# Query and key rows of an attention + mixture-of-experts block: loaded whole, by the sync queue, beside the expert tiles

## What is computed

```
x: [2, 1024, 256];  xn = layernorm(x)
y = x + attention(xn) + ffn(xn)
attention: qkv = xn @ qkv_w.T + qkv_b; 16 heads of 16; scores = q.k/4 + slope*(k_pos - q_pos), causal softmax; @ v; @ out_w.T + out_b
ffn: scores = sigmoid(xn @ gate_w); the top 2 of 16 experts by scores + expert_bias, weights normalised to sum 1
     shared  = (silu(xn @ sg_w) * (xn @ su_w)) @ sd_w
     routed  = sum over the two experts e of weight_e * ((silu(g) * u) @ experts_down[e]),  [g|u] = xn @ experts_gate_up[e]
     ffn     = shared + routed
```

## Time and profile before

| | us |
|---|---|
| median of 3 executions | 526.53 |
| lowest, highest | 524.24, 529.89 |
| the profiled execution | 525.04 |
| its span, first to last instruction | 523.2 |
| TensorE busy in it | 461.9 (88%) |
| VectorE busy | 324.3 (62%) |
| ScalarE busy | 249.4 (48%) |
| POOL busy | 198.4 (38%) |
| HBM read, written | 37.27 MB, 27.13 MB |

### The profile page before, as it was taken

One profiled execution on the slowest core, in us unless ns is written; L12 is line 12 of the kernel. 1 busy time (PEld: TensorE's weight loads), 2 busy tenths in 40 slices (PEclk: granted clock), 3 DMA queues, 4 the chain that ended last, 5 costly groups with the idle time before them and its releaser, 6 DMA issues.

```text
span 523.2 us, 9031 instructions
## 1 busy us (share of the span) xinstructions
PE 461.9 (88%) x3049; PEld 271.6 (52%) x3050; DVE 324.3 (62%) x610; ACT 249.4 (48%) x567; POOL 198.4 (38%) x239
## 2 busy tenths in 40 slices
PE   4595999737859999995999999999999999999998
PEld 4454788525635666763445354444444444332676
DVE  3869985413425656676867877778586867744232
ACT  2620652112213333332767676676676757678300
POOL 3470777699940000006888888800000000000000
PEclk9799799977779999997999999999999999999999
DMA  9898999799999434424113333221120000010022
GB/s 282 188 403 256 318 323 291 246 170 144 188 174 203 127 110 121 130 79 140 42 49 104 108 86 106 71 76 61 48 82 18 3 3 3 1 13 6 3 89 73
DMA packets 65705, 64.60 MB, mean 123 GB/s; under 512 B 21935, under 2 KB 59539, under 8 KB 65635
## 3 DMA queue, kind: packets, MB, share of 16 engines
q1 hardware_dynamic: 51506, 47.85, 30.9%
q0 software_dynamic: 13056, 15.83, 15.0%
q10 hardware_dynamic: 1104, 0.41, 0.3%
HBM read 37.27 MB, written 27.13 MB: 123 GB/s over the span
## 4 chain that ended last, share of the span: by engine, by line
PE 66%; DVE 13%; DMA 12%; issue 2%; ACT 2%; POOL 2%; SPq 1%; POOLq 0%; DVEq 0%
PE ps L1248 12%; PE ps L1222 10%; PE ps L1234 10%; PE ps L1147 7%; PE ps L1268 5%; DMA x_in<-sorted_tokens 5%; DVE mx L970 5%; PE ps L1043 4%; PE ps L1163 4%; DMA ks<-aux_rows 2%; PE ps L1237 2%; PE ps L1223 2%; PE ps L1137 2%; ACT pt L718 2%; DMA x_sb<-x 1%
## 5 line engine op out<-in xcount | busy, mean ns | idle before, releaser
L718 ACT ACTIVATE pt<-ps 128x512 f32<-128x512 f32 (+3 forms) x384 | 167.1, 494 | 79.7 <-PE ps L1237 55.2
L970 DVE TENSOR_REDUCE mx<-ps 128x1 f32<-128x384 f32 (+6 forms) x189 | 153.3, 863 | 52.4 <-PE ps L1223 51.1
L1248 PE MATMUL ps<-pt,vg 128*32 128x512 f32 (+3 forms) x768 | 71.9, 492 | 0.0
L575 POOL DMA_INDIRECT yg<-sorted_outputs,slot_i x32 | 32.0, 1000 | 94.2 <-DMA sorted_outputs<-y_out 85.4
L1147 PE MATMUL ps<-w_gu,hx 128*128 x192 | 58.3, 432 | 3.8 <-issue 2.2
L1234 PE MATMUL ps<-qs,ks 111*128 111x512 bf16 (+3 forms) x192 | 55.7, 331 | 3.7 <-DMA qs<-nr 3.0
L1234 PE MATMUL ps<-qk 111*128 111x512 bf16 (+3 forms) x192 | 54.9, 329 | 1.8 <-ACT pt L718 0.3
L935 DVE COPY y_out<-ps 128x256 f32<-128x256 f32 x48 | 20.4, 425 | 56.4 <-PE ps L1163 52.7
L1237 PE MATMUL ps<-cbf 128*128 128x128 bf16 x256 | 52.4, 221 | 0.0
L691 ACT ACTIVATE hx<-ps 128x384 f32<-128x384 f32 (+1 forms) x48 | 22.9, 477 | 61.3 <-PE ps L1137 58.6
L1222 PE MATMUL ps<-qk 108*128 108x512 bf16 (+3 forms) x192 | 50.2, 328 | 1.8 <-DVE mx L970 1.3
(11 more groups left out here) (175 smaller groups left out, 737.9 us busy)
## 6 DMA issues: line engine op xcount, KB each, us to landing
sorted_tokens<-y_out SPq DMA_DIRECT2D x12, 512.0 KB, 5.0
qk_parts<-parts SPq DMA_DIRECT2D x16, 384.0 KB, 3.5
x_in<-sorted_tokens SPq DMA_DIRECT2D x48, 128.0 KB, 2.7
sorted_outputs<-y_out SPq DMA_DIRECT2D x48, 128.0 KB, 1.7
w_gu<-e_gu SPq DMA_DIRECT2D x1, 2816.0 KB, 12.9
x_sb<-x SPq DMA_DIRECT2D x4, 512.0 KB, 8.4
w_dn<-e_dn SPq DMA_DIRECT2D x1, 2048.0 KB, 8.7
y<-x_sb SPq DMA_DIRECT2D x16, 128.0 KB, 1.7
```

The costliest lines, as they stand in the source:

```text
L575: g_.indirect_dma_start(out=yg[:, n % 4, :], out_offset=None, in_=ysd, in_offset=bass.IndirectOffsetOnAxis(ap=slot_i[:, k, t:t + 1], axis= ...
L718: sc.activation(pt[:, s % 4, j, lo:CH], bank(n % 3)[:, lo:CH], ACT.Exp).then_inc(s_exp, 1)
L970: last = v.reduce_max(dst, src, axis=AX.X)
L1248: ins = te.matmul(ps[32 * j:32 * j + 32, OUT_BANK * CH + lo:(OUT_BANK + 1) * CH], vg[:, par, kb, j, :], pt[:, s % 4, j, lo:CH], start=kb = ...
```

## The change

`load` becomes `load_piece(queue, g, piece)`, which issues one transfer of a whole row (all 1024 positions, 8 KB in a partition): a list `ROW_PIECES` numbers the eight of a group. The two halves' semaphores become one per group. SP issues the eight of group 0 after the second part of the gate/up weights and before it waits for the scattered tokens, behind waits for the last shared-expert product (`s_g1`) and the last job (`s_free`). The loop of SP over tiles is written out, and behind the store of each of the tiles 0 to 23 it issues one piece of the groups 1 to 3. POOL issues none any more, and its waits ahead of them go. Groups 4 to 7 are loaded by SP at the same place, with eight transfers instead of sixteen. TensorE waits once per group.

```diff
--- before.py
+++ after.py
@@ -314,8 +314,8 @@
         s_ga = [sem(f"rows_gathered{i}") for i in range(4)]
         s_gw = sem("rows_weighed")
         s_gad = sem("rows_added")
-        s_first = [[sem(f"first_half{half}_loaded{n}") for n in range(NBUF)] for half in range(2)]
-        s_ld = [[sem(f"half{half}_loaded{n}") for n in range(NBUF)] for half in range(2)]
+        s_first = [sem(f"first_rows_loaded{n}") for n in range(NBUF)]
+        s_ld = [sem(f"rows_loaded{n}") for n in range(NBUF)]
         s_vg = sem("vg_ready")
         s_fr = sem("first_max_scores_ready")
         s_ff = sem("first_max_scores_read")
@@ -360,23 +360,25 @@
         LOADS = 8
         SC = HD ** -0.5
 
-        def load(queue, side, g, half):
-
+        ROW_PIECES = [(side, t0, n) for side in range(2) for t0, n in ((0, 3), (3, 2), (5, 1), (AUX0, 0))]
+
+        def load_piece(queue, g, piece):
+
+            side, t0, n = ROW_PIECES[piece]
             dst, order = (q_buf, k_buf)[side][g % NBUF], (Q_PARTS, K_PARTS)[side]
-            done = (s_first, s_ld)[g // NBUF][half][g % NBUF]
-            cols = slice(half * CH, (half + 1) * CH)
-            for t0, n in ((0, 3), (3, 2), (5, 1)):
+            done = (s_first, s_ld)[g // NBUF][g % NBUF]
+            if n == 0:
+                rows = (N_ALIBI, N_AUX)[side]
+                queue.dma_start(dst[AUX0:AUX0 + rows, :, :],
+                                auxd[side, g:g + 1, :, 0:rows, :].rearrange("g j r s -> r (g j) s")
+                                ).then_inc(done, DMA)
+                return
+            if side == 0:
                 p0 = order[t0]
-                if side == 0:
-                    src = qkd[0, p0:p0 + 1, g:g + 1, :, :, cols].rearrange("n g d j s -> (g n) d j s")
-                    src = src.broadcast_to([n, HD, HG, CH])
-                else:
-                    src = qkd[1, 0:n, g:g + 1, :, :, cols].rearrange("n g d j s -> (g n) d j s")
-                queue.dma_start(dst[HD * t0:HD * (t0 + n), :, cols], src).then_inc(done, DMA)
-            rows = (N_ALIBI, N_AUX)[side]
-            queue.dma_start(dst[AUX0:AUX0 + rows, :, cols],
-                         auxd[side, g:g + 1, :, 0:rows, cols].rearrange("g j r s -> r (g j) s")
-                         ).then_inc(done, DMA)
+                src = qkd[0, p0:p0 + 1, g:g + 1].rearrange("n g d j s -> (g n) d j s").broadcast_to([n, HD, HG, S])
+            else:
+                src = qkd[1, 0:n, g:g + 1].rearrange("n g d j s -> (g n) d j s")
+            queue.dma_start(dst[HD * t0:HD * (t0 + n), :, :], src).then_inc(done, DMA)
 
         @block.sync
         def _(sp):
@@ -437,6 +439,11 @@
             sp.dma_start(w_gu[:, 0:E_LATE, :, :], e_gu[0:E_LATE].rearrange("e (c p) f -> p e c f", p=P)
                          ).then_inc(s_wgu, DMA)
 
+            sp.wait_ge(s_g1, 4)
+            sp.wait_ge(s_free, NJ)
+            for piece in range(LOADS):
+                load_piece(sp, 0, piece)
+
             sp.wait_ge(s_scat, K_TOP * TT * DMA)
 
             def load_tile(k, u):
@@ -460,10 +467,11 @@
 
             for k in range(4, 7):
                 next_tile(k, k % 4)
-            with sp.Fori(0, NT // 4 - 2) as i:
-                for u in range(4):
-                    next_tile(i * 4 + u + 7, (u + 3) % 4)
-                    store_tile(i * 4 + u, u)
+            for k in range(NT - 8):
+                next_tile(k + 7, (k + 3) % 4)
+                store_tile(k, k % 4)
+                if k < (NBUF - 1) * LOADS:
+                    load_piece(sp, 1 + k // LOADS, k % LOADS)
             next_tile(NT - 1, 3)
             for k in range(NT - 8, NT):
                 store_tile(k, k % 4)
@@ -479,9 +487,8 @@
                     store_neg(g + 1, (g + 1) % 2)
                 if g + NBUF < NG:
                     sp.wait_ge(s_st, (g + 1) * (HG * NS))
-                    for half in range(2):
-                        for side in range(2):
-                            load(sp, side, g + NBUF, half)
+                    for piece in range(LOADS):
+                        load_piece(sp, g + NBUF, piece)
 
             for g in range(NG):
                 sp.wait_ge(s_rec, max(0, g - (NG - 3)) + 1)
@@ -551,16 +558,6 @@
             pool.wait_ge(s_free, NJ)
             copy_v(0, 0)
             copy_v(1, 1)
-
-            pool.wait_ge(s_sh, TT // 2)
-            pool.wait_ge(s_auxst, 4 * DMA)
-            for i, stored in enumerate(s_parts):
-                pool.wait_ge(stored, DMA * len(range(i, NQK, RING)))
-            pool.wait_ge(s_scat, K_TOP * TT * DMA)
-            for g in range(NBUF):
-                for half in range(2):
-                    for side in range(2):
-                        load(pool, side, g, half)
 
             for u in range(4):
                 pool.wait_ge(s_ys[u], NT // 4 * DMA)
@@ -1165,8 +1162,8 @@
 
             def first_scores(j, q, n, first):
 
-                if first and n in (0, QT // 2):
-                    pe.wait_ge(s_first[n // (QT // 2)][0], LOADS * DMA)
+                if first and n == 0:
+                    pe.wait_ge(s_first[0], LOADS * DMA)
                 if not (first and n == 0):
                     pe.wait_ge(s_ff, n)
                 w = (q + 1) * P
@@ -1286,16 +1283,15 @@
                                 weigh(g + par - (a == 0), (a - back) % NS, par - (a == 0))
                         elif kind == "max" and not (last and a + par > 1):
                             n = g + par + a
-                            if b in (0, FIRST_HALF):
-                                pe.wait_ge((s_first, s_ld)[n // NBUF][int(b > 0)][n % NBUF], LOADS * DMA)
+                            if b == 0:
+                                pe.wait_ge((s_first, s_ld)[n // NBUF][n % NBUF], LOADS * DMA)
                             max_scores(n, n % 2, b)
                 for s in (NS - 2, NS - 1):
                     weigh(g + 1, s, 1)
                 return beside
 
 
-            for half in range(2):
-                pe.wait_ge(s_first[half][1], LOADS * DMA)
+            pe.wait_ge(s_first[1], LOADS * DMA)
             for p in range(EARLY):
                 max_scores(1, 1, p)
             for g in range(0, NG, 2):
```

## The result

| | median us | lowest, highest | executions |
|---|---|---|---|
| before | 525.38 | 523.81, 529.89 | 4 |
| changed | 564.85 | 564.33, 566.08 | 4 |

The changed kernel takes 1.074 times as long, with a 95% interval of 1.067 to 1.081: 39.5 us slower, where 20.5 had been forecast. The profiled execution of it has a span of 562.8 us against 523.2.

The account below looks back on a forecast made before the run. TensorE held two thirds of the chain, with transfers setting the pace between 99 and 160 us. Store 28 came 21 us later, the rest added zero: 525.04 + 21 = 546, on the median's scale 547; range 531 to 561.

Parts of the forecast that it names:

- The engine count: Sync-queue q/k loads: transfers of three or two repeats run on three or two of sixteen DMA engines; 23 us a group.
- step 2: Groups 1 to 3 beside 24 tiles: the most loaded DMA engine is the bound, 85.4 us, 3.6 us a tile.
- step 3: After the last piece: store 28 leaves about 2 us later, at 219 instead of 197.95, +21 us.
- step 1: Group 0 ahead of the tiles: drain from 98 to 121, first transposes 121.5 (+21 us), store 0 at 131.5.
- The tail: Tile steps 28 to 47: run as before, since nothing crowds them today.
- step 4: Groups 4 to 7, loaded beside attention: TensorE waits for no q/k row there; zero change.
- A: Whole q/k rows: all sixteen engines share them, 4.4 us a group; -20 us, 506.5; 9 in 100.
- B: Sync queue: tile loads overtake the q/k pieces; -9 us, 517; 3 in 100.
- C: Q/k loads: long runs are faster than allowed, 31 GB/s from an engine; time 527; 6 in 100.
- D: Sync queue: blocks on issue and stores slip behind pieces, 26 us a group; +35, 561; 12 in 100.
- The signs: Tile stage: DMA share some 0.2 with TensorE idle, transposes near 121, stores 3.6 us apart, tile-load waits 35 us or more.

Follow-up runs that it names:

- wide_all: Changed kernel with the sixteen dimensions outermost and repeats inside, in source and SBUF, for all eight groups; 507.92 us, ratio 0.968 to the kernel before.
- the ladder: Changed kernel, then the same with large transfers' outer source count raised to 4, 8 and 16; 564.85, then 534.4, 517.5 and 507.9 us.
- spread_40: Changed kernel with the 24 pieces of groups 1 to 3 behind 24 of the first 40 stores instead of the first 24; 565.80 us.
- one_big: Changed kernel with a two- or three-repeat piece behind every third or fourth store and a small one behind the next, over 40 stores; 559.35 us.
- group0_behind: Changed kernel with group 0 issued behind the first four tile loads instead of ahead of them; 556.91 us.
- lone_big: As one_big, but the twelve small pieces of groups 1 to 3 go behind the last eight stores; 560.71 us.

## Why the prediction was right in its direction and short in its size

**The engine count** was the whole argument, and it held: the earlier trace rows showed three and two engines, wide_all and the ladder prove it for the whole rows too. The mechanism was right. The time lies 4 us above the range, because terms of the sum were too small: above all the queue's 85.4 us of step 2, then the 2 us of step 3 and the start of step 1. Before to after by these marks:

| | predicted | measured |
|---|---|---|
| store 0 leaves (step 1) | 131.5 | 135.54 |
| from there until the queue is through with its pieces: landing of the load of tile 31 (step 2) | 85.4 | 94.5 |
| from there to store 28 (step 3) | 2 | 7.4 |
| store 28 leaves | 219 | 237.46 |

**Step 1**, short by 4. The first transposes came at 126.02 instead of 121.5. Of these 4.5 us, 2.1 are the profiled execution's own earlier stages (weights issued at 87.63 instead of 85.55), 1.3 a longer landing of the weights (14.2 instead of 12.9 us), and 1.1 the drain, 24.1 against 23 us. On its plateaus an engine ran faster than I took it, 27 GB/s, but not throughout: from 104 to 108 us a share of 0.19, three engines, moved only 58 GB/s. Store 0 then came 9.5 us later, where I had 10.

**Step 2**, short by 9, is the term that missed most. That the engine never runs dry and is the bound is borne out by the landings, which follow each other without a gap; the beat is 15.1 us for four tiles, 3.77 a tile, where I had 3.6. But a piece was priced at its bytes, 131 kB / 24 = 5.5 us and 0.3 for the load behind it. The first one took 10.8 us, 5 more; the other eleven took 66.5 us, 2.6 more; the tiles' own traffic makes the rest. Counting bytes per engine works while the pieces are packed. spread_40 and one_big show where it fails: with the queue empty in between, each piece of three repeats costs some 4 us more, and the mean load forecasts a gain that doesn't come.

**Step 3**, short by 5, let the load of tile 31 gate store 28, 2 us ahead of it. That load landed at 230.1, but the gate in the trace is the load of tile 29, the last one behind a large piece. From its landing at 228.15 to store 28 at 237.46 are three steps after a wait, at a granted clock of 0.57 from 230 to 235 us, 9.3 us in all. The pieces that end the queue are small, and TensorE, once let go, must still do every tile between the gate and the mark, at the lower clock first.

4 + 9.1 + 5.4 = 18.5, which is 237.46 - 219. The tail was right to 0.1 us, and **step 4** was right as well: no wait for a q/k row in attention.

**The rivals.** A's price was in effect a forecast of wide_all: 506.5, measured 507.92. That it came so near is in part luck: group 0 took 9.5 us there instead of 4.4 and store 0 left at 120.66 instead of 112.5, and the tiles behind it took 2.14 us instead of 2.34. For the changed kernel A did not happen; B did not either (group0_behind shows an order kept), nor C. D, with 561, was near in number only: its bubbles aren't in the landings.

**The signs** named at the end came true, with one proviso: DMA share 0.26 with TensorE idle, first transposes in the 120s, stores 3.7 us apart from store 5 to 28, no wait at the first scores. TensorE's waits on tile loads are 50.7 us where "35 or more" stood, but only with the first one; beside the pieces alone they are 25. Every term that missed, missed to the same side, and the range above 547 should have been the wider side.

## What to carry to other kernels

Before a transfer is moved to the sync queue, look at what rate that queue gives the same shape: a plateau that is a small multiple of the rate of one engine (here 27 GB/s) with a DMA share of a few sixteenths says that the outermost count of the source (3 or 2) sets the number of engines. The remedy is the order of the dimensions, not the place or the size of the transfer: with a count of 16 outermost the same moves went from 7% slower to 3% faster, and a count of 8 already had 47 of the 57 us. And price what stands ahead of a small, urgent transfer in the same queue as a delay to be set against its buffers' cover, one large piece at a time, not as a mean load. Where pieces can't be spread over all engines, spreading them in time isn't a way out: over 40 tiles instead of 24 they won nothing, or 1% at most.

## What the runs showed of the hardware that I had not expected

- With all sixteen engines on q/k rows (wide_all, share 0.99) only 185 GB/s moved, while the clearing stores moved 405 at the same share. So group 0 took about 9.5 us where 4.4 were reckoned. Each transfer there writes 16 to 48 partitions; whether that is the cause wasn't tried.
- A tile load right behind one three-repeat transfer with nothing large ahead landed 10.1 to 11.5 us after issue (one_big, lone_big), where the bytes ahead of it and its own landing make 7; behind other pieces the same transfer added only 6.0 to 6.9 us (changed kernel). Not explained.
- Each engine's rate fell when more of them worked on q/k rows: 27 GB/s with two and four, 25 with three, 14 to 20 with eight, 11.6 with sixteen.
- Longer runs did raise the rate of an engine where two to four of them worked: 24 GB/s with 1 KB, 25 to 27 with 8 KB.
